# Loading and normalising the input by the tile ahead of a fused attention and mixture-of-experts layer

## The reference

```python
def _layernorm(x, axis=-1, eps=1e-05):
    m = jnp.mean(x, axis=axis, keepdims=True)
    v = jnp.var(x, axis=axis, keepdims=True)
    return (x - m) / jnp.sqrt(v + eps)
# attention: x (4, 512, 512) fp32, 16 heads of 32, rotary q and k, causal softmax, output projection Wo
# ffn: 64 experts of width 128, top 8 of each token weighed by softmax, and one shared expert with a sigmoid gate
x = L0_attn_x
x = x + _layernorm(_L0_attn_ref(_layernorm(x), Wq, Wk, Wv, Wo))
x = x + _layernorm(_L0_ffn_ref(_layernorm(x), router_w, Wg, Wu, Wd, Wsg, Wsu, Wsd, Wse))
```

## Time and profile before

| what | value |
|---|---|
| median of 3 runs | 1215.02 us (1214.99 to 1217.04) |
| the profiled execution's own time | 1215.08 us |
| its span, first to last instruction | 1213.2 us |
| mean granted TensorE clock, share of full | 0.943 |
| busy: TensorE, VectorE, ScalarE, GpSimd | 1055.3, 702.6, 469.4, 628.7 us |
| attention begins its loop (first turn of block 0) | 36.96 us |

### The profile page before, as it was taken

How to read it: one execution, slowest core, us unless ns; L and a number is a source line. 1 busy time by engine, 2 the same in 40 slices (tenths; PEclk the granted TensorE clock), 3 DMA queues, 4 the chain that set the end, 5 groups by cost and what they waited for, 6 DMA issues and landing times.

```text
span 1213.2 us, 24246 instructions
## 1 busy us (share of the span) xinstructions
PE 1055.3 (87%) x6243; PEld 717.2 (59%) x6244; DVE 702.6 (58%) x2355; ACT 469.4 (39%) x1354; POOL 628.7 (52%) x633
## 2 busy tenths in 40 slices
PE   5799899899999989878879999999999999999300
PEld 3455566555666545546447777777777777777200
DVE  3666566556666668758845544545444544454287
ACT  1666566556666732242212222222222222222122
POOL 4333333333333312200138888888888888788534
PEclk9899999989999999889969999999999999999755
DMA  9600000000000061100339999999999999997592
GB/s 353 230 2 1 4 1 2 3 2 2 1 2 2 1 234 52 61 18 1 115 117 210 221 212 256 227 240 239 264 228 256 230 255 265 253 201 136 118 386 98
DMA packets 65968, 166.80 MB, mean 137 GB/s; under 512 B 15570, under 2 KB 16850, under 8 KB 65760
## 3 DMA queue, kind: packets, MB, share of 16 engines
q0 software_dynamic: 38816, 83.95, 31.3%
q1 hardware_dynamic: 27072, 81.88, 19.2%
HBM read 121.03 MB, written 62.65 MB: 151 GB/s over the span
## 4 chain that ended last, share of the span: by engine, by line
PE 69%; DMA 11%; DVE 10%; issue 4%; ACT 2%; POOL 2%; DVEq 0%; POOLq 0%; SPq 0%; ACTq 0%
PE ps L886 16%; PE ps L638 14%; PE ps L897 8%; DMA sum_rows<-x_t,idx 6%; PE ps L697 6%; PE ps L753 4%; PE ps L870 4%; PE ps L667 4%; PE ps L717 4%; DMA x_t<-x_rows,idx 3%; PE ps L789 2%; PE ps L652 2%; POOL sum_rows L420 1%; PE ps L769 1%; PE ps L805 1%
## 5 line engine op out<-in xcount | busy, mean ns | idle before, releaser
L886 PE MATMUL ps<-big,work 128*128 x1264 | 300.8, 381 | 0.0
L420 POOL DMA_INDIRECT sum_rows<-x_t,idx x157 | 250.1, 1593 | 51.1 <-issue 41.1
L886 PEld LDWEIGHTS ps<-big,work 128*128 128x128 f32 x1264 | 229.0, 191 | 24.9
L414 POOL DMA_INDIRECT x_t<-x_rows,idx x163 | 170.5, 1046 | 71.5 <-issue 30.8
L638 PE MATMUL ps<-big 128*128 128x384 f32 x512 | 180.5, 496 | 1.5 <-ACT big L483 1.1
L359 POOL TENSOR_TENSOR work<-qkv_all,rope_sb 128x256 f32<-128x256 f32 x64 | 46.7, 730 | 251.6 <-ACT qkv_all L488 251.5
L594 ACT ACTIVATE work<-ps 128x512 f32<-128x512 f32 x159 | 95.0, 597 | 198.4 <-PE ps L870 147.9
L897 PE MATMUL ps<-big,work 128*128 x314 | 161.1, 594 | 0.9 <-issue 0.7
L870 PEld LDWEIGHTS ps<-ident_sb,x_t 128*128 128x128 f32 x636 | 79.0, 143 | 101.9 <-issue 75.9
L970 DVE CUSTOM_DVE_ANT_0 ps<-ps,mask_sb 128x128 f32<-128x128 f32 (+3 forms) x256 | 120.8, 512 | 24.0 <-PE ps L667 23.4
L505 ACT ACTIVATE work<-ps,neg_max 128x128 f32<-128x128 f32 (+3 forms) x256 | 132.4, 528 | 4.3 <-DVE neg_max L970 3.2
(11 more groups left out here) (166 smaller groups left out, 1419.4 us busy)
## 6 DMA issues: line engine op xcount, KB each, us to landing
big<-experts SPq DMA_DIRECT2D x65, 768.0 KB, 14.7
sum_rows<-x_t POOLq DMA_DIRECT2D x4, 2048.0 KB
big<-sum_rows SPq DMA_DIRECT2D x6, 1024.0 KB, 11.0
x_sb<-x SPq DMA_DIRECT2D x4, 1024.0 KB, 15.2
x_rows<-work SPq DMA_DIRECT2D x16, 256.0 KB, 2.0
sum_rows<-attn_t POOLq DMA_DIRECT2D x2, 2048.0 KB
out<-x_sb SPq DMA_DIRECT2D x16, 256.0 KB, 2.1
x_t<-sum_rows SPq DMA_DIRECT2D x3, 1024.0 KB, 14.5
```

Of the source, the lines that this page charges most:

```text
L414: pool.indirect_dma_start(rows[:, q, :], None, x2_rows, bass.IndirectOffsetOnAxis(ap=idx[:, q, 0:1], axis=0), bounds_check=last_row, oob_i ...
L420: pool.indirect_dma_start(sum_rows[p], bass.IndirectOffsetOnAxis(ap=idx[:, q, 1:2], axis=0), y_sb[:, q, :], None, bounds_check=last_row, o ...
L886: mm = pe.matmul(ps[:, 2 + p, 0:GATEUP], rows_t[:, p, c, :], w_ring[:, slot, c * GATEUP:(c + 1) * GATEUP], start=(c == 0), stop=(c == DC - 1))
```

## The change

- x of batch 0 is loaded as four tiles, each with its own semaphore `s_x0[t]`; the identity stands behind tile 0 and the weights of group 0 behind tile 1.
- x of batches 1 to 3 is loaded next, ahead of the mask and of the weights of groups 1 to 3. These weights are split into group 1 (`s_wqkv1`) and groups 2 and 3 (`s_in[I_WQKV]`).
- VectorE makes statistics and reciprocal root by the tile: the statistics of tile t stand ahead of the scaling of tile t - 1. ScalarE adds EPS as the bias of its square root.
- The statistics of batches 1, 2 and 3 stand between the last normalisation of batch 0 and the first turns: batches 1 and 2 ahead of `take_qkt` of tile 0, batch 3 between `take_qkt` of tiles 0 and 1. ScalarE takes three square roots for them, one for each batch. One reciprocal is left for the 12 tiles.
- GpSimd does rope tiles 2 and 3 ahead of the zero fills, and these now wait for the last weights and not for x.
- TensorE waits for group 1's weights after `score(0, 0)`, and for the rest in the block i == TB (inside the loop, in every batch).
- The memset of EPS moves from behind attention to the start of VectorE's list.

```diff
         def _(sp):
-            sp.dma_start(x_sb[:, 0:TB, :], x_v[:, 0:TB, :]).then_inc(s_xin[0], 16)
+            sp.dma_start(x_sb[:, 0, :], x_v[:, 0, :]).then_inc(s_x0[0], 16)
             sp.dma_start(ident_sb[:, :], ident).then_inc(s_in[I_IDENT], 16)
+            sp.dma_start(x_sb[:, 1, :], x_v[:, 1, :]).then_inc(s_x0[1], 16)
             sp.dma_start(wqkv_sb[:, :, 0, :], wqkv[:, :, 0, :]).then_inc(s_in[I_WQKV0], 16)
-            for i in (I_ROPE, I_MASK):
-                sp.dma_start(*LOADS[i]).then_inc(s_in[i], 16)
-            sp.dma_start(wqkv_sb[:, :, 1:G, :], wqkv[:, :, 1:G, :]).then_inc(s_in[I_WQKV], 16)
+            for t in range(2, TB):
+                sp.dma_start(x_sb[:, t, :], x_v[:, t, :]).then_inc(s_x0[t], 16)
+            sp.dma_start(*LOADS[I_ROPE]).then_inc(s_in[I_ROPE], 16)
             for b in range(1, B):
                 sp.dma_start(x_sb[:, b * TB:(b + 1) * TB, :], x_v[:, b * TB:(b + 1) * TB, :]).then_inc(s_xin[b], 16)
+            sp.dma_start(*LOADS[I_MASK]).then_inc(s_in[I_MASK], 16)
+            sp.dma_start(wqkv_sb[:, :, 1, :], wqkv[:, :, 1, :]).then_inc(s_wqkv1, 16)
+            sp.dma_start(wqkv_sb[:, :, 2:G, :], wqkv[:, :, 2:G, :]).then_inc(s_in[I_WQKV], 16)
...
             rope_tile(1, 0, 1)
+            rope_tile(2, 0, 2)
+            rope_tile(3, 0, 3)
             pool.wait_ge(s_zero, 1)
-            for b in range(1, B):
-                pool.wait_ge(s_xin[b], 16)
+            pool.wait_ge(s_in[I_WQKV], 16)
...
-            rope_tile(2, 0, 2)
-            rope_tile(3, 0, 3)
...
-            root(0, 1, 1)
+            eps = small[:, 0, 3:4]
+            act.wait_ge(s_eps, 1)
+            for t in range(TB):
+                act.wait_ge(s_ln, t + 1)
+                act.activation(rstd[:, t:t + 1], moments[:, t, 1:2], ACT.Sqrt, bias=eps).then_inc(s_std, 1)
...
-            root(1, B, 3)
+            for b in range(1, B):
+                act.wait_ge(s_ln, TB + b)
+                act.activation(rstd[:, b * TB:(b + 1) * TB], moments[:, b * TB:(b + 1) * TB, 1], ACT.Sqrt, bias=eps).then_inc(s_std, 1)
...
-            pe.wait_ge(s_in[I_WQKV], 16)
             score(0, 0)
+            pe.wait_ge(s_wqkv1, 16)
...
+                    if i == TB:
+                        pe.wait_ge(s_in[I_WQKV], 16)
                     turn(k, i, 2)
...
-            moments_of_input(0, 1)
+            dve.memset(small[:, 0, 3:4], EPS).then_inc(s_eps, 1)
+
+            def moments_of_tile(m):
+                dve.bn_stats(stats[:, m, :], x_sb[:, m, :]).then_inc(s_moments, 1)
...
+            def scale_tile(t):
+                dve.wait_ge(s_std, t + 1)
+                dve.reciprocal(rstd[:, t:t + 1], rstd[:, t:t + 1]).then_inc(s_rstd, 1)
+                dve.wait_ge(s_rstd, t + 1)
+                norm_x(0, t)
+
             for t in range(TB):
-                norm_x(0, t)
-            for t in range(LEAD_QKT):
+                dve.wait_ge(s_x0[t], 16)
+                moments_of_tile(t)
+                dve.wait_ge(s_moments, t + 1)
+                dve.bn_aggr(moments[:, t, :], stats[:, t, :]).then_inc(s_ln, 1)
+                if t >= 1:
+                    dve.wait_ge(s_ln, t)
+                    scale_tile(t - 1)
+            dve.wait_ge(s_ln, TB)
+            scale_tile(TB - 1)
+
+            for b in range(1, B):
+                if b == B - 1:
+                    take_qkt(0, 0, 0)
+                dve.wait_ge(s_xin[b], 16)
+                for m in range(b * TB, (b + 1) * TB):
+                    moments_of_tile(m)
+                for m in range(b * TB, (b + 1) * TB):
+                    dve.wait_ge(s_moments, m + 1)
+                    ins = dve.bn_aggr(moments[:, m, :], stats[:, m, :])
+                ins.then_inc(s_ln, 1)
+            for t in range(1, LEAD_QKT):
                 take_qkt(t, 0, t)
-            moments_of_input(1, B)
+            dve.wait_ge(s_std, TB + B - 1)
+            dve.reciprocal(rstd[:, TB:TILES], rstd[:, TB:TILES]).then_inc(s_rstd, 1)
+            dve.wait_ge(s_rstd, TB + 1)
+            dve.wait_ge(s_ln, TB + B - 1)
             dve.wait_ge(s_in[I_MASK], 16)
...
-            dve.memset(small[:, 0, 3:4], EPS).then_inc(s_own, 1)
-            own[0] += 1
-            dve.wait_ge(s_own, own[0])
```

More of the change, by code:

```diff
@@ L174, in sandwich_kernel @@
         s_xin = [sem(f"s_xin{i}") for i in range(B)]
+        s_x0 = [sem(f"s_x0_{t}") for t in range(TB)]
+        s_wqkv1 = sem("s_wqkv1")
         s_moments = sem("s_moments")
+        s_eps = sem("s_eps")
         s_ln = sem("s_ln")
         s_std = sem("s_std")
+        s_rstd = sem("s_rstd")
         s_xn = sem("s_xn")
@@ L540, in _ @@
             every_batch(act, batch)
-            eps = small[:, 0, 3:4]
             for i in range(TILES + 3):
```

## The result

| | before | after |
|---|---|---|
| median of 6 runs each | 1215.51 us (1212.1 to 1217.04) | 1206.53 us (1204.42 to 1207.04) |
| ratio after to before | | 0.9926, 95% interval 0.9911 to 0.9941 |
| profiled execution, its span | 1215.08, 1213.2 us | 1204.42, 1202.6 us |
| first exp, first turn of block 0 | 36.37, 36.96 us | 29.11, 29.70 us |

The change is worth 9.0 us by the medians. The profiled execution of after happens to be its fastest, and its span is 10.6 us shorter.

The account below looks back on a forecast made before the run. Waits before attention's first turn, chiefly the other batches' statistics and Exp table load, were taken to bound the kernel; 9.2 us (1.2 start, 8.0 statistics) plus 1.5 clock gave 10.7, so 1204.3 us, range 1201.3 to 1207.8.

Parts of the forecast that it names:

- Statistics: Before attention: statistics of batches 1 to 3 made during the projections bring the first exp sooner, 8.0 us.
- Start by tiles: Kernel start: x of batch 0 by tiles starts projection 0 at 10.9, not 12.48; 1.2 us taken.
- my lower bound: Projection 0: if full clock comes at the same absolute moment as before, only 0.9 us of the start's gain is kept.
- (c): Kernel start: pieces land late, cutting gains nothing, projection 0 again at 12.4; gain 8.0 + 1.5, 1205.5 us; chance 0.10.
- The Trainium skill's rule on large transfers: Loads of x: 75% of peak needs at least 1 MiB per DMA; at half rate tile 2 comes some 1.5 us later.
- Clock: Block 0 of attention: full clock survives the shortened TensorE gap of 2.4 us; 1.5 us, bounds 0 and 1.8.
- rival (a): Gap before block 0: the clock falls in the short gap too; gain 9.2, 1205.8 us; chance 0.27.
- my 1.76: Block 0 of attention: its 6.85 us against 5.09 for the same block of the last batch at full clock.
- Rival (b): Loop entry: TensorE's first turn stalls 3.5 us and the clock likely falls; gain 8.1, 1206.9 us; chance 0.13.
- (d): First turn: group 1's weights come late and hold the loop; gain under 0, 1215 to 1220 us; chance 0.05 with kin.
- that cover: GpSimd: slack between the end of the zero fills and rope of the second group; 1.5 us forecast to remain.
- the 1.4 that I had allowed for the clock: Jumps back of the loop: two equal stalls priced 1.4 us apart, so plain +-1.4 us in the range.

Follow-up runs that it names:

- run 10: Changed kernel with all 12 tiles' statistics ahead of the first turn copy, ScalarE's three roots and Exp table load ahead of projection 3's copy: 1204.59 us, 0.9928.
- run 5: Changed kernel with x of batch 0 loaded and its statistics made in one piece, Sqrt table loaded as ScalarE's first instruction: 1205.50 us, 0.9926.
- Run 4: Changed kernel with ScalarE's roots of batch 0 placed between its copies of the transposed tiles: 1204.92 us, 0.9918.
- run 1: The repeat: the changed kernel again, unaltered: 1205.35 us, 0.9926.
- Run 3: Kernel before with only the start by tiles; other loads, statistics of batches 1 to 3 and GpSimd's order as before: 1215.60 us, 1.0008.
- run 2: Changed kernel with x of batch 0 loaded and its statistics made in one piece, Sqrt table not placed by hand: 1206.89 us, 0.9934.
- run 6: Changed kernel with ScalarE's roots between its copies, plus 11 filler transposes before tile 0 and 11 between tiles 0 and 1: 1209.74 us, 0.9961.
- Run 8: Changed kernel with 40 semaphore increments that nobody waits for at the head of TensorE's list: 1214.28 us, 1.0000.
- run 11: Changed kernel with ScalarE's roots between its copies, Sqrt table loaded first, and projection 0 ahead of tile 1's transposes: 1203.00 us, 0.9912.
- run 7: Changed kernel with 20 filler transposes in TensorE's gap between score 0 and the first turn: 1210.97 us, 0.9979.
- run 9: Kernel before with 16 semaphore increments that nobody waits for at the head of VectorE's list: 1214.26 us, 0.9998.
- run 12: Changed kernel with early statistics, roots and Exp table, roots between copies, Sqrt table first, projection 0 ahead of tile 1's transposes: 1201.08 us, 0.9901.

## Why the prediction was right, and where it was not

Forecast 1204.3 (1201.3 to 1207.8), measured 1206.5: 9.0 us against 10.7. The number held, the sum did so only in its largest term: the steps that I forecast gave 7.8 us in the profile and not 10.7. What brought the number nearer stands under "Not in the sum at all" and is luck. Step by step:

**Statistics, 8.0 us: right.** From the first turn of q and k to the first exp it was 13.5 us before and is 5.4 after, 8.1 less. The order (last copy, three roots, table load) came as written, VectorE's last aggregate and ScalarE's copy ended together, and the table load was late next; run 10 shows the last, run 5 that this part alone gives 1205.5.

**Start by tiles, 1.2 us: wrong in sign; the step that failed.** I wrote that "the transposed tile 0 (about 8)" is there, and worked through VectorE's and TensorE's orders, but not ScalarE's, where four roots stand ahead of the first copy. The copy of tile 0 so waited for the statistics of tile 3 and projection 0 began at 12.17, not 10.9. Run 4 puts the roots between the copies and has it at 11.34. The rest is the clock: I bounded projection 0 by its old 3.67 us, and it took 4.84 us (full clock only from its seventh pass, at 16.1, where before it was from the fourth, at 14.4) and 5.22. Full clock did not come at the old moment, as my lower bound had it, but later. Together the start costs 0.86 in the profile, 0.5 in the repeat, where I had put a gain of 1.2. Run 3 (first exp 1.2 later) agrees; its time can't be used for it, as said there. Of my rivals (c), no gain at the start, came nearest, though the pieces landed about on time: tiles 0 and 1 were ready at 3.5 and 5.2, tile 2 at 8.85, the last x at 17.9 (forecast 4.2, 5.0, 8.2, 17.3). The Trainium skill's rule on large transfers (page "DMA: Bandwidth & Descriptors", section Bandwidth), which I had weighed there, is not borne out as the main cause. The cut did cost some rate (191 and 224 GB/s in the windows 3 to 4 and 4 to 5, against 356 and 414 before), and tile 2 was ready between 8.09 and 9.61 in the profiles with a cut start; it was late by 0.6 us in run 4, which accounts for its 11.34 against my 10.9.

**Clock, 1.5 us: mis-sized, and rival (a) is what happened.** The gap was 2.34 us, as forecast at 2.4, but the clock fell all the same, 0.2 us behind the first turn, and block 0 became only 0.5 us shorter than 6.85. The 4.9 us at full clock in the old gap misled me. Eight profiles have this gap of 2.34 us (after and runs 1, 2, 4, 5, 6, 8 and 11). Only run 4 kept full clock; in the others it fell between 0.3 us ahead of the first turn and 2.6 us behind it, and block 0 took 6.34 to 7.80 us. Why run 4 was spared stays open. Full clock would have been worth 5.54 to 5.67 (runs 4 and 7) against 6.85, so 1.2 to 1.3; the 5.09 of the last batch, from which my 1.76 came, was not reached in any of them.

**Rival (b), a stall at loop entry: false.** TensorE's first turn starts 0.59 us after the first exp (29.11, 29.70), as in the kernel before (36.37, 36.96). **(d), late weights: false.** The first turn is released by the exp, and GpSimd's zero fills, which wait for the last weights, follow rope without a wait for a transfer (30.11). So all weights were there by 30.1. (The 6080 KB that I gave as ahead of group 1's weights include them.) The fills ended at 33.9 and rope of the next group waited 2.45 us for its input, so that cover held, by more than the 1.5 I gave it.

**Not in the sum at all:** VectorE's stalls (1.05 us) and the jumps back (1.98 us in this pair of profiles; I had put them in the range as a matter of the clock). Without these the profile would have shown 7.6. The first follows the place of VectorE's code (run 9), which the change shifted. Of the second, about 1.3 us is the clock in the one profile of before (runs 3 and 9), so the 1.4 that I had allowed for the clock there was right in kind; some 0.3 us is left at the second jump back (16.12 and 16.23 from block 31 to 33 with the old TensorE list; 15.66 to 16.35, in the mean 15.86, with the new one in the changed kernel and runs 1, 2, 4, 5 and 10), and nothing clear at the first. Run 8 shows that code alone can do as much; whether it did here stays open. An estimate from these rows, 7.8 + 1.05 + 0.3, gives 9.2 us, near the medians' 9.0 and, in run 1, 9.6. The medians don't resolve a microsecond, so that is as far as it goes.

## What to carry to other kernels

When work is cut into pieces to start sooner, follow the first piece through the queue of every engine: one list that still takes all pieces before its next kind of work (here ScalarE's four roots) gives the gain away. Where a table load belongs to the first activation, place it by hand ahead of the waits. And before a difference of a few microseconds is put down to an edit, compare the distance between equal events of both profiles, since code that only shifts can cost as much as an edit wins.

## What the runs showed of the hardware

- 40 instructions that do nothing, ahead of a hardware loop on TensorE, took the time from 1206 to 1214 us: the two jumps back cost 3.1 and 5.6 us more, with a second stall of 0.7 us in the scores behind the jump and 0.8 and 2.0 us of it as a longer time at half clock. 16 on VectorE's list removed a stall of 0.36 us in each of three passes of its loop.
- The granted clock fell to half in seven of eight profiles with a gap of 2.34 us on TensorE, mostly when it already worked again, and stayed full in run 4; 20 transposes in the gap held it full. It fell after 1.22 us in run 10 and not after 1.32 us in run 12.
- The clock column read 1.00 in the first 28 us of every profile here, while passes of projection 0 were 0.64 us apart, the distance that goes with 0.50 later on.
- A table load that the program doesn't place stood at 0.73 us in the kernel before and at 4.52 or 9.10 once a second wait was added ahead of the same activation.
